# Thirty-eight passes written out without a loop, and the second attention's weights loaded in two halves

## The chip, the cores and the metric

One core of a Trainium2 chip runs the whole kernel. The metric is the device time of one execution in microseconds (us), as the median of several runs. The engines are TensorE (PE), VectorE (DVE), ScalarE (ACT), GpSimd (POOL) and SyncE (SP), which issues every DMA of this kernel. The sixteen DMA engines serve SP's one queue.

## The reference

A batch of 32 sequences of 256 tokens with 128 features goes through two transformer layers. Each half of a layer ends in a layer norm after the residual.

```
x = layernorm(x + L0_attn(x))   # 16 heads of 8, softmax over all 256 keys, distance bias
x = layernorm(x + L0_ffn(x))    # 8 experts, top 2 by softmax gate, plus one shared expert
x = layernorm(x + L1_attn(x))   # no full softmax: each token looks back at fixed offsets
x = layernorm(x + L1_ffn(x))    # 8 experts, one matrix each, top 2
```

The part that the change touches is the sum of the second attention, here with T = 256 and the offsets that are smaller than T:

```
for i, off in enumerate(OFFSETS):      # sorted, distinct, under 256: 16 of them
    vs = v shifted down by off
    out = out + attn[..., i] * vs      # attn has one weight per head, token and offset
out = (out * sigmoid(x @ w_gate + b_gate)) @ w_out + b_out
```

## The kernel before

**Passes.** The kernel is a software pipeline by hand. A sequence goes through the stages A1 and M (scores and their maxima, first attention), A2 and A3 (probabilities, output), B and B2 (first experts), C1 and C2 (second attention), D and D2 (second experts). Each stage lags by some passes (`LAG`, 0 to 6), so that in pass t the stage with lag k works on sequence t - k. There are 38 passes (t = 0 to 37). Every engine goes through its own list of steps (`ORDER`) in each pass, in that order, and waits on semaphores at each step. The `Steps` class counts them.

**The loop.** Passes 0 to 6 are written out. Passes 7 to 30 run in a loop of 12 rounds with two passes in its body, an odd one and an even one (`passes`, L286 to L295; `LOOP_FROM` is 7, `LOOP_TO` is 31). Passes 31 to 37 are written out again. So there are 11 jumps back, each between an even pass and the odd one after it: 8 to 9, 10 to 11, up to 28 to 29. The written-out passes 5 and 6 do the same work as those in the loop, but for the last experts' sums (D2), which begin in pass 6.

**The start of a pass.** On PE a pass begins with A1.qk (L423, L424). ACT turns its result into the highest of three bfloat16 parts (L668, L670). DVE makes the other two (L911, L915). SP stores the three (`d_parts<-parts`, L337) and loads them back as rows of the scores' stack with 12 DMAs (`stack<-d_parts`, L345 and L350), which wait for the stores. The score matmuls A1.S (L559, first of a pass: A1.S.0) need the stack. DVE takes the four norms' inverse roots together (N.root, L817 to L834). ACT applies them (L754), and PE transposes the results (L441).

**The weights of the second attention.** At the end of C1 the weights lie transposed in `wT`. SP stores them to DRAM (C1.dw, L374), then M.m (L384) goes out, and then SP loads `wb` with one DMA of 2048 KB (C1.wb, L380): each of the 128 partitions gets all 16 offsets of its head, 16 KB. In the next pass DVE multiplies offset pairs with shifted values (C2.pv.0 to .7, L923). Only pv.0 waits for the load. The pairs are taken in the order 0, 1, 4, 5, 2, 3, 6, 7 (`PV_ORDER`). DVE's list around them:

```
N.root.0 N.root.1 N.root.2 N.root.3 C2.pv.0 C2.pv.1 C2.pv.2 C2.pv.3
C2.pv.4 G.rank C2.pv.5 G.weigh C2.pv.6 C2.pv.7 A1.max.0 C2.add.0 ...
```

G.rank begins with a copy from PSUM (L845) of the gates' logits that PE makes at L458. POOL folds the sixteen products in two steps (C2.add, L1070): step 0 after the fourth product adds offsets 8 to 11 to 0 to 3, step 1 after the last adds 12 to 15 to 4 to 7. DVE folds the rest (L969, L974, L981) and applies the gate (L987).

**SP's list** of a pass:

```
A1.part.0 A3.x A1.part.1 A1.part.2 A1.rows.0 A1.rows.1 A1.rows.2 B.cT B.cb X.xT D.cT D2.out D.cb C1.dw M.m C1.wb
```

Of the kernel before, what the change touches and what calls it, by code (L numbers as in the profile page):

```python
# [6 lines left out]
B, T, D = 32, 256, 128  # L7
H, HD = 16, 8
# [30 lines left out]
LAST = max(LAG.values())  # L39
LOOP_FROM = LAST + 1  # L40
LOOP_TO = LOOP_FROM + (B - 1 - LOOP_FROM) // 2 * 2
Z_FIRST = 6
PV_ORDER = (0, 1, 4, 5, 2, 3, 6, 7)

# [22 lines left out]
        A1.part.0 A3.x A1.part.1 A1.part.2 A1.rows.0 A1.rows.1 A1.rows.2 B.cT B.cb X.xT D.cT D2.out D.cb C1.dw M.m  # L67
        C1.wb""",
}
# [31 lines left out]
def network(nc, A, out):  # L101
# [4 lines left out]
    with ctx:  # L106
# [139 lines left out]
        st_cB, ld_cB, st_cD, ld_cD = sem("st_cB"), sem("ld_cB"), sem("st_cD"), sem("ld_cD")  # L246
        st_w, ld_w, st_out = sem("st_w"), sem("ld_w"), sem("st_out")
        setup_dve, setup_act = sem("setup_dve"), sem("setup_act")
# [36 lines left out]

        def passes(eng, one):  # L286


            for t in range(LOOP_FROM):
                one(t, t % 2, t)  # L290
            with eng.Fori(0, (LOOP_TO - LOOP_FROM) // 2) as r:
                for u in range(2):
                    one(r * 2 + (LOOP_FROM + u), (LOOP_FROM + u) % 2, LOOP_FROM + u)
            for t in range(LOOP_TO, B + LAST):
                one(t, t % 2, t)  # L295
# [5 lines left out]
        def _(sp):  # L301
# [15 lines left out]
            def one(t, par, key):  # L317
                r = stages(t)
                for what, n in ORDER["sp"]:
# [3 lines left out]
                    if what == "X.xT" and (e := r["X"]) is not None:  # L323
                        sp.wait_ge(peA1.sem, peA1.count(e - 1, "v"))
                        sp.dma_start(xT[:], A["xT"][:, bass.ds(e * T, T)]).then_inc(ld_xT, 16)
                    if what == "A3.x":
                        if (e := r["A3"]) is not None:
                            sp.wait_ge(dveA3.sem, dveA3.count(e - 1, "res"))
                            sp.dma_start(x0[:], x_rows[:, bass.ds(e * TT, TT), :]).then_inc(ld_x, 16)
                    if what == "A1.part" and (e := r["A1"]) is not None:  # L330
# [39 lines left out]
                    if what == "C1.dw" and (e := r["C1"]) is not None:  # L370

                        sp.wait_ge(ld_w, dma_count(e - 1))
                        sp.wait_ge(actC1.sem, actC1.count(e, "wT"))
                        sp.dma_start(bass.AP(d_w.tensor, 0, [[T, 8], [NS * T, H], [8 * T, 2], [1, T]]),  # L374
                                     wT[:]).then_inc(st_w, 16)
                    if what == "C1.wb" and (e := r["C1"]) is not None:

                        sp.wait_ge(st_w, dma_count(e))
                        sp.wait_ge(dveC2.sem, dveC2.count(e - 1, "gt"))
                        sp.dma_start(wb[:].rearrange("p s n -> p (s n)"),  # L380
                                     bass.AP(d_w.tensor, 0, [[NS * T, H], [0, HD], [1, NS * T]])).then_inc(ld_w, 16)
                    if what == "M.m" and (e := r["M"]) is not None:
                        sp.wait_ge(actM.sem, actM.count(e, "mT"))
                        sp.dma_start(stack[par][ROW_M:ROW_M + 1, 0], mT[:]).then_inc(ld_m, 16)  # L384
                    if what == "D2.out" and (e := r["D2"]) is not None:
                        sp.wait_ge(actND.sem, actND.count(e, "nm", 1))
                        sp.dma_start(out_rows[:, bass.ds(e * TT, TT), :], xout[:]).then_inc(st_out, 16)

            passes(sp, one)
            sp.wait_ge(st_out, dma_count(B - 1))  # L390


        @block.tensor
        def _(pe):
# [14 lines left out]
            def one(t, par, key):  # L409
                if key == LOOP_FROM and not isinstance(t, int):  # L410
                    for b in last:
                        last[b] = (*last[b][:4], t - 1)
                if isinstance(t, int) and t == LOOP_TO:
                    for b in last:
                        last[b] = (*last[b][:4], LOOP_TO - 1)
                r = stages(t)
# [215 lines left out]

            passes(pe, one)


        @block.scalar
        def _(act):
# [129 lines left out]

            passes(act, one)


        @block.vector
        def _(dve):
# [116 lines left out]
            def one(t, par, key):  # L889
# [6 lines left out]
                for what, n in ORDER["dve"]:  # L896
# [20 lines left out]
                    if what == "C2.pv" and (e := r["C2"]) is not None:  # L917

                        if n == 0:
                            dve.wait_ge(ld_w, dma_count(e))  # L920
                            dve.wait_ge(actC1.sem, actC1.count(e, "v"))
                        p = PV_ORDER[n]
                        v.tensor_tensor(pv[:, 2 * p:2 * p + 2, :], wb[:, 2 * p:2 * p + 2, :], shifted(vC, p),  # L923
# [42 lines left out]
                    if what == "C2.add" and n == 0 and (e := r["C2"]) is not None:  # L966

                        dve.wait_ge(poolC2.sem, poolC2.count(e, "add", 1))
                        v.tensor_tensor(pv[:, 0:4, :], pv[:, 0:4, :], pv[:, 4:8, :], ALU.add).then_inc(dveC2.done("add", 0), 1)  # L969
                    if what == "N.root" and n == 1 and present:  # L970
# [77 lines left out]

            passes(dve, one)


        @block.gpsimd
        def _(pool):
# [4 lines left out]
            def one(t, par, key):  # L1058
                r = stages(t)
                odd = 1 - par  # L1060
                for what, n in ORDER["pool"]:
# [5 lines left out]
                    if what == "C2.add" and (e := r["C2"]) is not None:  # L1067

                        pool.wait_ge(dveC2.sem, dveC2.count(e, "pv", 4 * n + 3))
                        tt_(pv[:, 4 * n:4 * n + 4, :], pv[:, 4 * n:4 * n + 4, :], pv[:, 4 * n + 8:4 * n + 12, :],  # L1070
                            ALU.add).then_inc(poolC2.done("add", n), 1)
# [34 lines left out]

            passes(pool, one)

# [116 lines left out]
```

## Time and profile before

| | |
|---|---|
| median of 3 runs | 2006.53 us (1998.36 to 2018.55) |
| the profiled execution | 2014.43 us, of which 2012.6 us span |
| PE busy | 1601.7 us (80%) |
| DVE busy | 1334.9 us (66%) |
| ACT and POOL busy | 922.6 us, 917.0 us (46% each) |
| DMA moved | 214.15 MB, mean 106 GB/s |

No engine is busy throughout. The span runs from the first instruction to the last. In the rows below, a bracket at the end of a row of the timeline tells how long the engine was idle before the instruction and what ended that. "issue" means that it waited for nothing that the profile shows. Rows of SP are the moments at which DMAs were issued, not their transfer.

### The profile page before, as it was taken

The page shows a single profiled execution, that of the slowest core. Times are in us where ns is not written, and L with a number is a line of the kernel's source. Part 1 is how long each engine was busy: PE and PEld are TensorE (multiplying, and loading weights), DVE is VectorE, ACT ScalarE, POOL GpSimd, SP SyncE. Part 2 cuts the span into 40 slices and gives each one's busy share as a digit, 9 for nine tenths or more (in the row PEclk, how much of TensorE's full clock was granted, in tenths as well). Part 3 has the DMA queues.
Part 4 walks back from the last instruction along what each step waited for, and adds up shares of the span by engine and source line. Part 5 has one row for each costly group of instructions (what it writes and reads, how often), then busy time and mean ns, then how long its engine had stood idle before and what let it go on. Part 6 is the DMA issues. An engine that isn't in the chain of part 4 may idle for free.

```text
span 2012.6 us, 41817 instructions
## 1 busy us (share of the span) xinstructions
PE 1601.7 (80%) x12928; PEld 1209.2 (60%) x12928; DVE 1334.9 (66%) x3466; ACT 922.6 (46%) x1868; POOL 917.0 (46%) x772
## 2 busy tenths in 40 slices
PE   1788888887888888888878878888888888886633
PEld 1466666665666666566666656666666666664523
DVE  2456777776757767576767767677677767775543
ACT  1355444454545445454535545554455545543310
POOL 0014355455535554553555455355545554455542
PEclk9899989898989989899989898999899989998755
DMA  5334444354544434454443444444344445433321
GB/s 102 86 90 106 95 113 109 98 125 107 129 107 117 115 91 115 102 128 107 118 113 94 112 107 129 109 120 118 87 112 123 115 118 128 106 95 92 92 71 50
DMA packets 86025, 214.15 MB, mean 106 GB/s; under 512 B 11634, under 2 KB 68210, under 8 KB 68594
## 3 DMA queue, kind: packets, MB, share of 16 engines
q1 hardware_dynamic: 85844, 211.96, 42.6%
q8 instruction: 87, 1.43, 0.4%
q14 instruction: 94, 0.77, 0.2%
HBM read 185.97 MB, written 25.69 MB: 105 GB/s over the span
## 4 chain that ended last, share of the span: by engine, by line
PE 33%; issue 20%; POOL 15%; DMA 13%; DVE 10%; ACT 5%; SPq 3%; DVEq 0%; POOLq 0%; ACTq 0%
POOL prod L1079 7%; DMA d_parts<-parts 6%; DMA stack<-d_parts 5%; PE b L521 4%; PE bPV L542 3%; POOL h L1104 3%; DVE mx L1005 3%; PE bS L559 3%; PE bTU L571 3%; POOL prod L1095 3%; PE bTU L572 2%; PE b L580 2%; PE bTU L491 2%; POOL wb L1070 2%; PE bPV L510 2%
## 5 line engine op out<-in xcount | busy, mean ns | idle before, releaser
L1005 DVE TENSOR_REDUCE mx<-bS 128x2 f32<-128x512 f32 x512 | 337.0, 684 | 204.9 <-PE bS L562 202.4
L1079 POOL TENSOR_TENSOR prod<-kC,qC 128x512 f32<-128x512 f32 x256 | 363.7, 1451 | 142.2 <-ACT kC L683 142.2
L1104 POOL TENSOR_TENSOR h<-ub,gBcb 128x256 f32<-128x256 f32 x256 | 185.1, 729 | 422.3 <-DVE ub L1018 370.3
L1070 POOL TENSOR_TENSOR wb<-wb 128x1024 f32<-128x1024 f32 x64 | 162.6, 2541 | 417.3 <-DVE wb L923 417.3
L714 ACT ACTIVATE P<-bTU 128x512 f32<-128x512 f32 x512 | 276.8, 606 | 27.6 <-PE bTU L494 22.4
L559 PE MATMUL bS<-stack 96*128 96x256 bf16 x1024 | 232.8, 296 | 65.9 <-DMA stack<-d_parts 21.5
L723 ACT ACTIVATE sil<-bTU,b 128x256 f32<-128x256 f32 x288 | 136.7, 474 | 299.5 <-PE bTU L572 134.2
L571 PE MATMUL bTU<-x1T,w 128*128 128x256 f32 x576 | 203.5, 437 | 50.5 <-DVE h L1018 49.9
L491 PE MATMUL bTU<-stack 97*128 97x256 bf16 x1024 | 237.8, 284 | 4.9 <-ACT P L714 3.8
L494 PE MATMUL bTU<-dist,identh 128*128 128x128 f16 x1024 | 213.0, 226 | 0.0
L562 PE MATMUL bS<-dist,identh 128*128 128x128 f16 x1024 | 210.2, 233 | 0.0
L923 DVE TENSOR_TENSOR wb<-wb,vC 128x512 f32<-128x512 f32 x256 | 174.0, 731 | 45.1 <-DMA wb<-d_w 44.7
L559 PEld LDWEIGHTS bS<-stack 96*128 96x128 bf16 x1024 | 106.7, 104 | 154.2 <-DVE mx L1005 68.6
L572 PE MATMUL bTU<-x1T,w 128*128 128x256 f32 x576 | 185.3, 405 | 0.0
L1095 POOL TENSOR_TENSOR prod<-gDcb,x3T 128x512 f32<-128x512 f32 x128 | 160.6, 1267 | 34.1 <-DMA gDcb<-d_cD 34.1
L542 PE MATMUL bPV<-w,h 128*128 128x128 f32 x1152 | 154.0, 287 | 19.8 <-POOL h L1104 19.8
L521 PE MATMUL b<-ew,prod 128*128 128x128 f32 x1024 | 147.6, 299 | 17.1 <-POOL prod L1095 17.1
L542 PEld LDWEIGHTS bPV<-w,h 128*128 128x128 f32 x1152 | 143.7, 201 | 25.0 <-POOL h L1104 24.8
L521 PEld LDWEIGHTS b<-ew,prod 128*128 128x128 f32 x1024 | 135.5, 211 | 24.7 <-POOL prod L1095 14.3
L510 PE MATMUL bPV<-P,Vz 128*32 128x256 f32 x2048 | 148.0, 410 | 0.7 <-ACT P L714 0.7
L571 PEld LDWEIGHTS bTU<-x1T,w 128*128 128x128 f32 x576 | 94.1, 204 | 67.1 <-DVE h L1018 57.2
L491 PEld LDWEIGHTS bTU<-stack 97*128 97x128 bf16 x1024 | 106.1, 104 | 40.6 <-ACT P L714 26.4
(159 smaller groups left out, 2909.2 us busy)
## 6 DMA issues: line engine op xcount, KB each, us to landing
wb<-d_w SPq DMA_DIRECT2D x32, 2048.0 KB, 12.5
gBcb<-d_cB SPq DMA_DIRECT2D x32, 1024.0 KB, 4.8
gDcb<-d_cD SPq DMA_DIRECT2D x32, 1024.0 KB, 4.7
stack<-d_parts SPq DMA_DIRECT2D x288, 64.0 KB
stack<-d_parts SPq DMA_DIRECT2D x96, 192.0 KB
d_parts<-parts SPq DMA_DIRECT2D x96, 128.0 KB, 7.7
d_w<-wT SPq DMA_DIRECT2D x32, 256.0 KB
xT<-in_xT SPq DMA_DIRECT2D x32, 128.0 KB, 4.6
```

The lines of the kernel that those rows point to most:

```text
L491: mm(o[:, q], stack[odd][0:ROW_M + 1, 1, h, kt * 128:kt * 128 + 128], stack[odd][0:ROW_M + 1, 0, h, :], start=True, stop=False)
L494: i = mm(o[:, c], identh[:], dist[:, h, 0, :], start=False, stop=last_part)
L521: i = mm(b6[:, tt * 128:tt * 128 + 128], xs[:, x, tt * 128:tt * 128 + 128], ew[:, x, :], start=(x == 0), stop=(x == E - 1))
L542: i = mm(bPV[:, tt * 128:tt * 128 + 128], h9[:, x, tt * 128:tt * 128 + 128], w2[:, expert(x), :], start=False, stop=(x == E), skip_group_c ...
L559: mm(o[:, qt * T:qt * T + T], stack[par][0:ROW_M, 0, h, qt * 128:qt * 128 + 128], stack[par][0:ROW_M, 1, h, :], start=True, stop=False)
L571: mm(bAB[:, 0:T], w13[:, x, 0, :], x1T[:], start=True, stop=True)
L572: mm(bAB[:, T:2 * T], w13[:, x, 1, :], x1T[:], start=True, stop=True).then_inc(peB.done("ab", n), 1)
L714: act_f(P[k % 8][:].rearrange("p a b -> p (a b)"), bTU[turn_bank("ST", k)][:], ACT.Exp).then_inc(actA2.done("exp", k), 1)
L1005: v.tensor_reduce(mx[:, :, k], bS[k % 2][:].rearrange("p (a b) -> p a b", a=TT), op=ALU.max, axis=AX.X).then_inc(dveA1.done("max", k), 1)
L1079: tt_(prod[:, 2 * p:2 * p + 2, :], shifted(kC, p), qC[:].unsqueeze(1).to_broadcast([128, 2, T]), ALU.mult).then_inc(poolC1.done("prod", p), 1)
L1095: tt_(xs[:, 2 * i:2 * i + 2, :].rearrange("p x (t n) -> p x t n", t=TT), gD["cb"][:, :, 2 * i:2 * i + 2, :].rearrange("p t x n -> p x t n" ...
L1104: tt_(h9[:, n, :].rearrange("p (t n) -> p t n", t=TT), ub[n % 2][:].rearrange("p (t n) -> p t n", t=TT), gB["cb"][:, :, expert(n), :], ALU ...
```

## The change

1. The loop goes. `passes` writes all 38 passes out on each of the five engines. With it go the loop registers in DMA addresses and wait values, and the fix-ups of PE's bank bookkeeping at the loop's edges.
2. The load of `wb` is two DMAs of 1024 KB, offsets 0 to 7 (C1.wb.0) and 8 to 15 (C1.wb.1), issued one behind the other, each with its own semaphore. A partition's row is now 8 KB in each. DVE waits for the first half before pv.0 and for the second before pv.4.
3. `PV_ORDER` goes: the products are taken in the order 0 to 7. POOL's step 0 adds offsets 4 to 7 to 0 to 3, its step 1 adds 12 to 15 to 8 to 11, and DVE's first fold adds 8 to 11 to 0 to 3.
4. SP's wait before C1.dw is on the last product of the sequence before (pv 7), in place of the load of `wb`.

```diff
-        C1.wb""",
+        C1.wb.0 C1.wb.1""",
...
-        def passes(eng, one):
-
-
-            for t in range(LOOP_FROM):
-                one(t, t % 2, t)
-            with eng.Fori(0, (LOOP_TO - LOOP_FROM) // 2) as r:
-                for u in range(2):
-                    one(r * 2 + (LOOP_FROM + u), (LOOP_FROM + u) % 2, LOOP_FROM + u)
-            for t in range(LOOP_TO, B + LAST):
+        def passes(one):
+
+            for t in range(B + LAST):
                 one(t, t % 2, t)
...
-                        sp.wait_ge(ld_w, dma_count(e - 1))
+                        sp.wait_ge(dveC2.sem, dveC2.count(e - 1, "pv", 7))
                         sp.wait_ge(actC1.sem, actC1.count(e, "wT"))
...
-                        sp.wait_ge(st_w, dma_count(e))
-                        sp.wait_ge(dveC2.sem, dveC2.count(e - 1, "gt"))
-                        sp.dma_start(wb[:].rearrange("p s n -> p (s n)"),
-                                     bass.AP(d_w.tensor, 0, [[NS * T, H], [0, HD], [1, NS * T]])).then_inc(ld_w, 16)
+                        if n == 0:
+                            sp.wait_ge(st_w, dma_count(e))
+                            sp.wait_ge(dveC2.sem, dveC2.count(e - 1, "gt"))
+                        sp.dma_start(wb[:, 8 * n:8 * n + 8, :].rearrange("p s n -> p (s n)"),
+                                     bass.AP(d_w.tensor, 8 * n * T,
+                                             [[NS * T, H], [0, HD], [1, 8 * T]])).then_inc(ld_w[n], 16)
...
+                        p = n
+                        if n % 4 == 0:
+                            dve.wait_ge(ld_w[n // 4], dma_count(e))
                         if n == 0:
-                            dve.wait_ge(ld_w, dma_count(e))
                             dve.wait_ge(actC1.sem, actC1.count(e, "v"))
-                        p = PV_ORDER[n]
...
-                        v.tensor_tensor(pv[:, 0:4, :], pv[:, 0:4, :], pv[:, 4:8, :], ALU.add).then_inc(dveC2.done("add", 0), 1)
+                        v.tensor_tensor(pv[:, 0:4, :], pv[:, 0:4, :], pv[:, 8:12, :], ALU.add).then_inc(dveC2.done("add", 0), 1)
...
-                        tt_(pv[:, 4 * n:4 * n + 4, :], pv[:, 4 * n:4 * n + 4, :], pv[:, 4 * n + 8:4 * n + 12, :],
+                        tt_(pv[:, 8 * n:8 * n + 4, :], pv[:, 8 * n:8 * n + 4, :], pv[:, 8 * n + 4:8 * n + 8, :],
                             ALU.add).then_inc(poolC2.done("add", n), 1)
```

## Rows read from the trace of the kernel before

**Rows 1.** The page, its first line and PE's and DVE's busy time.

```profile
span 2012.6 us, 41817 instructions
...
PE 1601.7 (80%) x12928; PEld 1209.2 (60%) x12928; DVE 1334.9 (66%) x3466; ACT 922.6 (46%) x1868; POOL 917.0 (46%) x772
```

**Rows 2.** Waits: who waited for whom: us in total, times, longest us.

```profile
PE b L423 <- issue: 26.6, 6, 5.0
...
DVE n_v L817 <- issue: 14.7, 5, 4.1
...
PE bS L559 <- DMA stack<-d_parts: 21.5, 13, 7.2
...
DVE wb L923 <- DMA wb<-d_w: 44.7, 21, 6.8
...
DVE gL L845 <- PE b L458: 74.1, 30, 4.4
```

**Rows 3.** Timeline of PE, starts of passes 6, 7, 8, 9, 30, 31.

```profile
287.62 0.59 PE L423 MATMUL b<-xT,wqk 128*128 128x256 f32 x2
...
343.15 0.59 PE L423 MATMUL b<-xT,wqk 128*128 128x256 f32 x2
...
402.01 0.59 PE L423 MATMUL b<-xT,wqk 128*128 128x256 f32 x2
...
460.28 1.22 PE L423 MATMUL b<-xT,wqk 128*128 128x256 f32 x2 [4.00 <-issue]
...
1678.22 0.59 PE L423 MATMUL b<-xT,wqk 128*128 128x256 f32 x2
...
1733.41 0.59 PE L423 MATMUL b<-xT,wqk 128*128 128x256 f32 x2
```

**Rows 4.** Windows: us; busy PE, PEld, DVE, ACT, POOL; clock, DMA share, GB/s.

```profile
343.20:402.00 58.80, 51.38 (x405) 38.79 (x404) 40.30 (x106) 28.61 (x58) 28.71 (x24) 0.88 0.46 111
...
804.70:866.40 61.70, 51.72 (x406) 38.89 (x405) 40.27 (x107) 28.61 (x58) 28.82 (x24) 0.86 0.43 105
...
1564.50:1617.70 53.20, 46.01 (x406) 34.81 (x406) 40.93 (x106) 28.73 (x58) 28.87 (x24) 1.00 0.48 121
...
402.00:1678.20 1276.20, 1079.83 (x8889) 818.90 (x8888) 902.17 (x2311) 631.20 (x1276) 632.59 (x528) 0.93 0.45 112
```

**Rows 5.** Timeline, DVE and then PE, behind the jump back into pass 15.

```profile
818.75 0.17 DVE L817 TENSOR_SCALAR n_v<-n_mv 128x8 f32<-128x8 f32 x1 [4.12 <-issue]
...
823.17 0.47 PE L441 MATMUL b<-ident,x 128*128 128x128 f32 x1 [4.59 <-ACT x L754]
```

**Rows 6.** Timeline of SP from 860 to 900 us, start of pass 16.

```profile
867.78 0.56 SPq L380 DMA_DIRECT2D wb<-d_w  x1
869.13 0.37 SPq L337 DMA_DIRECT2D d_parts<-parts  x1
...
880.32 3.80 SPq L345 DMA_DIRECT2D stack<-d_parts  x9
```

**Rows 7.** Timeline of PE, pass 16: first score matmul.

```profile
893.66 0.28 PE L559 MATMUL bS<-stack 96*128 96x256 bf16 x1 [0.99 <-DMA stack<-d_parts]
```

**Rows 8.** Timeline of DVE, pass 16: five products, then the gate's logits.

```profile
880.12 3.10 DVE L923 TENSOR_TENSOR wb<-wb,vC 128x512 f32<-128x512 f32 x5 [1.19 <-DMA wb<-d_w]
884.95 0.19 DVE L845 COPY gL<-b 128x32 f32<-128x32 f32 x1 [1.73 <-PE b L458]
```

**Rows 9.** DMA issues: times, KB each, median us from issue to landing.

```profile
wb<-d_w SPq DMA_DIRECT2D x32, 2048.0 KB, 12.5
gBcb<-d_cB SPq DMA_DIRECT2D x32, 1024.0 KB, 4.8
...
stack<-mT SPq DMA_DIRECT2D x32, 8.0 KB, 2.2
```

**Rows 10.** Timeline of PE in pass 4, DVE in passes 33 and 34.

```profile
202.76 0.39 PE L559 MATMUL bS<-stack 96*128 96x256 bf16 x1 [0.16 <-DMA stack<-d_parts]
...
1904.95 3.10 DVE L923 TENSOR_TENSOR wb<-wb,vC 128x512 f32<-128x512 f32 x5 [2.58 <-DMA wb<-d_w]
...
1955.76 3.10 DVE L923 TENSOR_TENSOR wb<-wb,vC 128x512 f32<-128x512 f32 x5 [4.38 <-DMA wb<-d_w]
```

More of the change, by code:

```diff
@@ L246, in network @@
         st_cB, ld_cB, st_cD, ld_cD = sem("st_cB"), sem("ld_cB"), sem("st_cD"), sem("ld_cD")
-        st_w, ld_w, st_out = sem("st_w"), sem("ld_w"), sem("st_out")
+        st_w, ld_w, st_out = sem("st_w"), [sem(f"ld_w{n}") for n in range(2)], sem("st_out")
         setup_dve, setup_act = sem("setup_dve"), sem("setup_act")
@@ L324, in one @@
                         sp.wait_ge(peA1.sem, peA1.count(e - 1, "v"))
-                        sp.dma_start(xT[:], A["xT"][:, bass.ds(e * T, T)]).then_inc(ld_xT, 16)
+                        sp.dma_start(xT[:], A["xT"][:, e * T:e * T + T]).then_inc(ld_xT, 16)
                     if what == "A3.x":
@@ L328, in one @@
                             sp.wait_ge(dveA3.sem, dveA3.count(e - 1, "res"))
-                            sp.dma_start(x0[:], x_rows[:, bass.ds(e * TT, TT), :]).then_inc(ld_x, 16)
+                            sp.dma_start(x0[:], x_rows[:, e * TT:e * TT + TT, :]).then_inc(ld_x, 16)
                     if what == "A1.part" and (e := r["A1"]) is not None:
@@ L386, in one @@
                         sp.wait_ge(actND.sem, actND.count(e, "nm", 1))
-                        sp.dma_start(out_rows[:, bass.ds(e * TT, TT), :], xout[:]).then_inc(st_out, 16)
-            passes(sp, one)
+                        sp.dma_start(out_rows[:, e * TT:e * TT + TT, :], xout[:]).then_inc(st_out, 16)
+            passes(one)
             sp.wait_ge(st_out, dma_count(B - 1))
@@ L409, in one @@
             def one(t, par, key):
[L410 to L415, printed above, removed]
                 r = stages(t)
@@ L631, in one @@
                         i.then_inc(peM.done("mT"), 1)
-            passes(pe, one)
+            passes(one)
         @block.scalar
@@ L766, in one @@
                         nc.scalar.copy(mT[:], b7[:].bitcast(BF)[0:H, 0:T]).then_inc(actM.done("mT"), 1)
-            passes(act, one)
+            passes(one)
         @block.vector
@@ L1047, in one @@
                         v.tensor_scalar(mneg[:], mx[:], -1.0, None, ALU.mult).then_inc(dveM.done("neg"), 1)
-            passes(dve, one)
+            passes(one)
         @block.gpsimd
@@ L1105, in one @@
                             gB["cb"][:, :, expert(n), :], ALU.mult).then_inc(poolB.done("h", n - 1), 1)
-            passes(pool, one)
+            passes(one)
 def distance_tables():
```

3 lines of the change are left out of this document (removed).

## The prediction

> **What bounds the kernel now.** I read the page first. PE is busy 80% of the 2012.6 us, DVE 66%, and no engine is full [rows 1]. So the end is set by chains between engines and not by one engine's load, and I need to know what a pass costs and why passes differ. The starts of passes on PE give that. Passes 8 to 29 take 1276.2 us [rows 4], and 1276.2 / 22 = 58.0 us each. Four passes have no jump back at their start: pass 6 takes 343.15 - 287.62 = 55.5, pass 7 takes 58.9, pass 30 takes 55.2, and pass 8 takes 58.3 of which 4.0 is a stall at the jump that ends it, so 54.3 without [rows 3].
>
> The list of waits names the difference. PE stands still before the first matmul of a pass with the reason "issue" 26.6 us in 6 cases, and DVE before the norms' roots 14.7 us in 5 cases [rows 2]. 6 + 5 is 11, the number of jumps back. Around pass 15 the reader sees how such a stall goes on: DVE waits 4.12 us for nothing, the norms come late, and PE idles 4.59 us before it can transpose their results [rows 5]. That pass has a granted clock of 0.86 and takes 61.7 us. A pass with the clock at 1.00 takes 53.2 [rows 4]. So a stall can cost twice, once by itself and once by the clock that falls after PE's pause.
>
> Next I ask what limits a pass without a stall. In pass 16 the load of wb is issued at 867.78 and the store of the first parts at 869.13, behind it on the same queue. The rows of the stack can't be issued before 880.32 [rows 6]. PE waits the last 0.99 us before its first score matmul at 893.66 for the stack [rows 7]. The load of wb takes 12.5 us to land [rows 9], 867.78 + 12.5 = 880.3. So the first half of a pass is a chain of three DMA stages, and PE's own work is only about 1 us shorter. Over the run PE waits 21.5 us in 13 cases there [rows 2].
>
> **Part 1, the loop goes.** What goes is 11 jumps on five engines. The visible stalls are 26.6 + 14.7 = 41.3 us [rows 2]. I don't take that as the price, since a stall also moves the clock and since part of DVE's stall lies beside other work. I take the difference of whole passes: the mean of the four without a jump at their start is (55.5 + 58.9 + 54.3 + 55.2) / 4 = 56.0, against 58.0. That is 2.0 us in each of 22 passes, 45 us with the unrounded means (58.01 - 55.97). The two ways agree, which is why I trust the place. The ends: passes 6 and 7, which follow each other, average 57.2, and that gives only 22 x 0.8 = 18 us. The shortest pass of 53.2 gives 22 x 4.8 = 106 us, but it has no drop of the clock at all, so I hold it for out of reach.
>
> What it adds is code to fetch in a straight line. The written-out passes 6 and 30 to 31 show no stall at their starts [rows 3], so I cost it at nothing. The cover is that PE runs behind its queue. Without it a pass would stall about 4 us, as at a jump. The Trainium skill says the same (Runtime: NRT & Kernel Launch, section "Instruction fetch mechanics"): fetch ahead is sequential, and a taken branch to code outside the two pages at hand has to wait for a DMA. The trace agrees at the 11 jumps. By that page's sentence that runtime control flow costs and full unrolling is preferred, the gain would be all of the stalls; the sum above does not use it.
>
> **Part 2, the load in halves.** The bytes are the same. SP gets one more issue of 0.56 us [rows 6]. In pass 16 it would end at 867.78 + 2 x 0.56 = 868.9, before the store of the parts at 869.13, which waits for ACT. So it costs nothing there, with 0.2 us to spare. What lands when is not shown by any row. From below: gBcb, also with rows of 8 KB, lands 1024 KB in 4.8 us [rows 9], and two of these are 9.6, so 2.9 us sooner than now. From above: the second half pays a fixed part of its own, which a load of 8 KB shows as 2.2 us [rows 9], and waits 0.56 us to be issued. That would be 2.8 us later. I take 0 for the whole, because the source is the same (16 rows, each read by 8 partitions) and so the nearest row is wb itself.
>
> The first half then lands some 5 us before the second ((12.5 - 2.2) / 2, an estimate from [rows 9]), and pv.0 waits for nothing. In pass 16 that takes away 1.19 us on DVE. But the next thing DVE waits for is PE's logits, 1.73 us [rows 8], so it just waits there 1.2 us longer. This holds for the run: DVE waits 44.7 us for wb and right behind it 74.1 us for the logits [rows 2]. pv.4 needs the second half. It starts four products after pv.0, at 0.62 us each (3.10 / 5 [rows 8]) 2.5 us later, and so hides a second half that is up to 2.5 us late. POOL's first fold comes 1.2 us earlier, and then waits longer for the keys that ACT writes (its next step). In passes 4 and 5 pv.0 waits long, but PE starts its scores in pass 4 with the stack 0.16 us late [rows 10], so the stack caps the gain there. In passes 33 and 34, with no stack to load, pv.0 waits 2.58 and 4.38 us [rows 10]; of each at most the 2.5 us of four products goes. I take 5 us for both.
>
> **Part 3, the rest.** The order of products, the folds' addresses and SP's other wait change no size and no count. POOL's first fold still comes after the fourth product, its second after the last. The product pv 7 that SP now waits for is made long before wT is ready. All nothing.
>
> **Sum.** The profiled execution took 2014.4 us (span 2012.6 and 1.8 around it). 2014.4 - 45 - 5 = 1964.4. That execution lay 0.4% above the median of the three runs, so I scale by 2006.5 / 2014.4: 1957 us, 2.5% under the median of before.
>
> The skill's fit for one DMA is 2.0 us and the bytes at 436 per ns (DMA: Bandwidth & Descriptors, section "Anatomy of one DMA", written for GpSimd's path). It would make one load of 2048 KB 6.8 us and two loads that don't overlap 8.8 us, and the sum by it would be 2.0 us worse in each of 28 passes, 56 us. This trace has 12.5 us for that load, so the fit doesn't hold for it.
>
> **Rivals.**
> - *A, straight passes are no better than 6 and 7 together* (57.2). For it: pass 7 has no jump at its start, yet its clock is 0.88 and it takes 58.8 [rows 4]. Against it: pass 30 and pass 8. Gain 18 + 5: 1991.4, scaled 1984.
> - *B, the halves land sooner.* If wb lands 1 us earlier or more, the stack's wait of 0.99 us [rows 7] goes too, and PE's own order is next. 28 passes (4 to 31) have both loads: 28 more, 1936.4, scaled 1929. For it: gBcb's rate [rows 9]. Against it: another source pattern.
> - *C, the halves land later, and it ends slower.* Place: the store of the parts behind the two loads, in 28 passes. Price: up to 2.2 + 0.56 = 2.8 us each, and nothing hides it, since the stack already comes last [rows 7]. 28 x 2.8 = 78: 1964.4 + 78 = 2042.4, scaled 2034. It decides from 50 / 28 = 1.8 us of lateness on. The fit of the skill in the paragraph above is this rival's reason; its measured counterpart is the 2.2 us of a small load, and loads issued close together overlap that now (9 leave SP in 3.8 us [rows 6]).
> - *D, straight code doesn't take the stalls away*: they come back at other places of the 24 passes. Against it: the written-out passes. About 2002 to 2010.
>
> **Chances.** Forecast (1938 to 1978, a loop worth 25 to 65 us) 0.58; A 0.17; B 0.12; C 0.07; D 0.06. About 1% is what a measurement of this kernel can tell from no change, so the border is 1986. A lies on it, and I count half of it as faster. Faster: 0.58 + 0.09 + 0.12 = 0.79. Same: 0.08 of A, 0.05 of D, 0.02 of C = 0.15. Slower: 0.05 of C, 0.01 of D = 0.06. The range 1925 to 1992 holds the forecast, A and most of B. C and D lie outside.
>
> **What would show each step.** Right: no wait "issue" at the first matmul of a pass or at the norms' roots, passes 8 to 29 at 56 us on the mean, DVE's wait for wb near 0 outside the first passes, its wait for the logits grown by as much, PE's wait for the stack at 0 to 2 us. Wrong: the parts' store lands later than 14 us after the start of a pass (C), or sooner than 12 (B). The forecast fails most likely on the clock: if every straight pass drops to 0.88 as pass 7 does, the stalls are gone and half of the gain with them.

## The result, and the profile after

The changed kernel takes 1915.86 us (median of 4 runs, 1911.24 to 1918.87) against 2011.99 us for the kernel before in the same comparison (1998.36 to 2018.55, 4 runs). The ratio is 0.953, with a 95% interval of 0.947 to 0.959. That is 4.7% faster. The forecast was 1957, with 1925 to 1992 around it, so the direction was right and the gain was nearly twice the size: 96 us where 49 were expected.

The page first: the span, and the busy time of each engine with its share and its instructions.

```profile
span 1914.8 us, 36356 instructions
...
PE 1550.4 (81%) x12928; PEld 1176.4 (61%) x12928; DVE 1321.2 (69%) x3466; ACT 921.7 (48%) x1868; POOL 917.2 (48%) x772
```

The engines do the same work, instruction for instruction (compare the counts in [rows 1]). PE's busy time is 51 us less, at a granted clock of 0.935 of full speed over the span where before had 0.905. The rest of the gain is time in which PE stood still. Passes 8 to 29 are one window, from the first PE matmul of pass 8 to that of pass 30 (columns as in [rows 4]: us, then busy PE, PEld, DVE, ACT, POOL, then clock, DMA share, GB/s):

```profile
392.30:1588.00 1195.70, 1038.58 (x8889) 792.06 (x8888) 897.02 (x2311) 630.60 (x1276) 634.25 (x528) 0.96 0.48 120
```

1276.2 us in [rows 4] became 1195.7, so 80.5 of the 97.8 us between the two spans were won in these 22 passes, 54.35 us each in place of 58.01. The same windows laid over the ends give 227.6 to 215.9 us for passes 4 to 7, and 279.2 to 271.0 us from pass 31 to the end.

The list of waits has no "issue" any more at a pass's first matmul or at the norms' roots, where [rows 2] has 26.6 and 14.7 us. What it has instead (who waited for whom: us in total, times, longest us):

```profile
DVE gL L832 <- PE b L445: 85.8, 32, 3.7
...
PE bS L546 <- DMA stack<-d_parts: 60.8, 25, 7.9
```

PE's wait for the stack has grown from 21.5 us to 60.8. And DVE's wait for `wb`, 44.7 us before, is nearly gone. Its row in the list of instruction groups (out<-in, shape, count, then busy us and mean ns, then the idle time just before and what ended it):

```profile
L911 DVE TENSOR_TENSOR wb<-wb,vC 128x512 f32<-128x512 f32 x256 | 169.5, 711 | 8.7 <-DMA wb<-d_w 8.7
```

One pass shows what this means. In pass 20, which starts at 1046.56, SP issues both halves together, the store of the parts behind them, and the stack's rows 10.7 us after the first store (start us, us, line, times):

```profile
1047.85 1.18 SPq L372 DMA_DIRECT2D wb<-d_w  x2
1049.26 0.40 SPq L328 DMA_DIRECT2D d_parts<-parts  x1
...
1059.92 3.00 SPq L336 DMA_DIRECT2D stack<-d_parts  x9
```

PE is ready for its scores 1.90 us before the stack is:

```profile
1046.56 0.59 PE L410 MATMUL b<-xT,wqk 128*128 128x256 f32 x2
...
1074.23 0.28 PE L546 MATMUL bS<-stack 96*128 96x256 bf16 x1 [1.90 <-DMA stack<-d_parts]
```

So in this pass the chain of DMAs on SP's queue sets when the scores begin. In pass 16 DVE starts its products at once and waits for PE's logits instead, 2.76 us where [rows 8] has 1.19 for `wb` and 1.73 for the logits:

```profile
842.04 3.10 DVE L911 TENSOR_TENSOR wb<-wb,vC 128x512 f32<-128x512 f32 x5
847.90 0.19 DVE L832 COPY gL<-b 128x32 f32<-128x32 f32 x1 [2.76 <-PE b L445]
```

### The profile page after: what moved, and what is told of

Read it like the earlier page. It is cut to its first block, busy times and chain, and to the rows that moved or that the text cites. A ratio compares the mean times of both kernels' runs of the same rounds, so it can differ in the third digit from the quotient of the medians.

```text
span 1914.8 us, 36356 instructions
## 1 busy us (share of the span) xinstructions
PE 1550.4 (81%) x12928; PEld 1176.4 (61%) x12928; DVE 1321.2 (69%) x3466; ACT 921.7 (48%) x1868; POOL 917.2 (48%) x772
## 4 chain that ended last, share of the span: by engine, by line
PE 34%; DMA 30%; DVE 17%; issue 7%; SPq 6%; ACT 4%; POOL 3%; DVEq 0%; POOLq 0%; ACTq 0%
DMA d_parts<-parts 14%; DMA stack<-d_parts 13%; DVE mx L993 7%; PE bPV L529 5%; PE bS L546 4%; PE bTU L558 4%; SPq L336 4%; PE b L567 3%; PE bTU L559 3%; DVE wb L962 2%; DVE wb L957 2%; PE b L508 2%; PE bS L549 2%; DMA d_w<-wT 1%; POOL prod L1067 1%
## 5 line engine op out<-in xcount | busy, mean ns | idle before, releaser
L546 PE MATMUL bS<-stack 96*128 96x256 bf16 x1024 | 239.0, 301 | 97.6 <-DMA stack<-d_parts 60.8
L558 PE MATMUL bTU<-x1T,w 128*128 128x256 f32 x576 | 207.4, 445 | 41.2 <-DVE h L1006 40.8
L478 PE MATMUL bTU<-stack 97*128 97x256 bf16 x1024 | 227.0, 275 | 4.6 <-ACT P L701 3.6
L549 PE MATMUL bS<-dist,identh 128*128 128x128 f16 x1024 | 215.5, 237 | 0.0
L481 PE MATMUL bTU<-dist,identh 128*128 128x128 f16 x1024 | 206.5, 220 | 0.0
L559 PE MATMUL bTU<-x1T,w 128*128 128x256 f32 x576 | 188.1, 411 | 0.0
L911 DVE TENSOR_TENSOR wb<-wb,vC 128x512 f32<-128x512 f32 x256 | 169.5, 711 | 8.7 <-DMA wb<-d_w 8.7
L529 PE MATMUL bPV<-w,h 128*128 128x128 f32 x1152 | 148.3, 279 | 19.8 <-POOL h L1092 19.8
L529 PEld LDWEIGHTS bPV<-w,h 128*128 128x128 f32 x1152 | 136.9, 192 | 26.1 <-POOL h L1092 25.9
L497 PE MATMUL bPV<-P,Vz 128*32 128x256 f32 x2048 | 138.0, 387 | 0.7 <-ACT P L701 0.7
L559 PEld LDWEIGHTS bTU<-x1T,w 128*128 128x128 f32 x576 | 120.1, 209 | 19.5
L558 PEld LDWEIGHTS bTU<-x1T,w 128*128 128x128 f32 x576 | 96.0, 208 | 58.5 <-DVE h L1006 47.6
```

The source lines that it names most:

```text
L478: mm(o[:, q], stack[odd][0:ROW_M + 1, 1, h, kt * 128:kt * 128 + 128], stack[odd][0:ROW_M + 1, 0, h, :], start=True, stop=False)
L481: i = mm(o[:, c], identh[:], dist[:, h, 0, :], start=False, stop=last_part)
L529: i = mm(bPV[:, tt * 128:tt * 128 + 128], h9[:, x, tt * 128:tt * 128 + 128], w2[:, expert(x), :], start=False, stop=(x == E), skip_group_c ...
L546: mm(o[:, qt * T:qt * T + T], stack[par][0:ROW_M, 0, h, qt * 128:qt * 128 + 128], stack[par][0:ROW_M, 1, h, :], start=True, stop=False)
L549: i = mm(o[:, c], identh[:], dist[:, h, 0, :], start=False, stop=True)
L558: mm(bAB[:, 0:T], w13[:, x, 0, :], x1T[:], start=True, stop=True)
```

## The experiments

Eleven kernels ran, each timed beside the kernel before. They came in three groups with a median of before each (2008.42, 2017.62 and 2020.49 us), and the changed kernel was timed in a fourth (2011.99), so ratios are compared across groups and medians within one. The time of a pass is the window of passes 8 to 29 divided by 22. Windows, waits and spans come from one profiled execution of each kernel, ratios from all its runs. All of them compute the whole reference.

**The two parts apart.** The first takes the load in halves out of the changed kernel and leaves the loop gone; the other way round the second keeps the loop and has the halves. The third is the changed kernel, but DVE waits for both halves before its first product.

Straight passes only, against the changed kernel (against the kernel before, nothing but the loop is gone):

```diff
-        C1.wb.0 C1.wb.1""",
+        C1.wb""",
...
+                        sp.wait_ge(ld_w, dma_count(e - 1))
...
+                        sp.dma_start(wb[:].rearrange("p s n -> p (s n)"),
+                                     bass.AP(d_w.tensor, 0, [[NS * T, H], [0, HD], [1, NS * T]])).then_inc(ld_w, 16)
...
+                        p = PV_ORDER[n]
```

> The kernel before with its 38 passes written out and nothing else changed: one load of wb, the old order of products. Theory L (the loop is all of it, the forecast only mis-sized the gain of a straight pass): about 1920 us, passes 8 to 29 at 54.4 us as in the changed kernel. Theory H (the halves take part in every pass, because pv.0 starts at 12.2 us in a pass where it started at 13.7 behind the load): about 1957 us, passes at 56.0 us, DVE waiting for wb about 1 us in every pass.

Halves in the loop, against the kernel before (the load, the order and the folds as in the change, and SP waits for both loads where it waited for the one):

```diff
-                        sp.wait_ge(ld_w, dma_count(e - 1))
+                        for half in range(2):
+                            sp.wait_ge(ld_w[half], dma_count(e - 1))
```

> The kernel before, loop kept, with the load in two halves, the two semaphores and the new order of products (SP waits for both halves before C1.dw, since the wait on pv 7 isn't used here). Theory L: 2007 us, the 5 us of the first and last passes. Theory H: in each of the 12 even passes of the loop, in which pv.0 waits for wb now, 1.6 us or more go, so 1980 us or less.

Wait for both, against the changed kernel:

```diff
-                        if n % 4 == 0:
-                            dve.wait_ge(ld_w[n // 4], dma_count(e))
                         if n == 0:
+                            for half in range(2):
+                                dve.wait_ge(ld_w[half], dma_count(e))
```

> The changed kernel, but DVE waits for both halves before pv.0. The two DMAs, the order and the straight passes stay. Theory L: at most 5 us slower than the changed kernel, 1916 to 1921. Theory H: about 1950 us, since pv.0 is back at 13.7 us in a pass.

Straight passes alone took 1947.45 us, ratio 0.969 (0.962 to 0.976). Halves in the loop took 1991.16 us, 0.990 (0.982 to 0.998). The wait for both took 1936.29 us, 0.963 (0.956 to 0.971). None of the three came out as either theory had it: each lies between L (1920, 2007, at most 1921 us) and H (1957, at most 1980, 1950). The windows of the same 22 passes, one fence for each kernel in that order:

```profile
395.90:1605.30 1209.40, 1039.01 (x8890) 791.78 (x8889) 910.43 (x2311) 632.87 (x1276) 636.91 (x528) 0.97 0.49 119
```

```profile
396.90:1667.60 1270.70, 1067.48 (x8890) 813.90 (x8889) 898.77 (x2311) 630.56 (x1276) 631.74 (x528) 0.94 0.45 113
```

```profile
394.00:1591.80 1197.80, 1035.21 (x8890) 788.91 (x8889) 902.54 (x2311) 632.77 (x1276) 637.98 (x528) 0.97 0.49 120
```

A straight pass costs 54.97 us with one load, so the loop alone was worth (58.01 - 54.97) x 22 = 67 us by the profiles, and 61 by the medians (2008.42 - 1947.45). The halves add 32 us on top: (0.969 - 0.953) x 2012. By the profiled spans it is 1944.8 - 1914.8 = 30.0, of which 13.7 lie in passes 8 to 29, 6.0 in passes 4 to 7 (221.9 against 215.9 us) and 11.6 from pass 31 on (282.6 against 271.0); the other passes together lose 1.3. With the loop kept the halves bring 0.010 x 2012 = 20 us, and of these only 1276.2 - 1270.7 = 5.5 in passes 8 to 29.

The third kernel splits that again. It has the two DMAs but not DVE's early start, and in its profiled execution it is within 2.1 us of the changed kernel in passes 8 to 29, and within 0.3 us in passes 4 to 7 (216.2 against 215.9). So what the halves bring there comes from when the bytes land and not from when DVE begins. From pass 31 on it needs 279.9 us against 271.0, so the early start counts at the end. By the spans the early start is worth 1926.6 - 1914.8 = 11.8 us of the 30.0. But the profiled execution is the fastest of this kernel's four (1928.41 to 1941.22), and by the ratios it is (0.963 - 0.953) x 2012 = 20 us of the 32. Where the slower executions lose the difference isn't known. At the end there is no stack to load, and DVE waits (timeline of DVE near the end, first the changed kernel, then the one that waits for both):

```profile
1811.24 3.16 DVE L911 TENSOR_TENSOR wb<-wb,vC 128x512 f32<-128x512 f32 x5
...
1856.47 2.50 DVE L911 TENSOR_TENSOR wb<-wb,vC 128x512 f32<-128x512 f32 x4 [1.10 <-DMA wb<-d_w]
```

```profile
1869.15 3.10 DVE L911 TENSOR_TENSOR wb<-wb,vC 128x512 f32<-128x512 f32 x5 [5.51 <-DMA wb<-d_w]
```

When do the bytes land? The table has, for each of the 22 passes, the time from the pass's first PE matmul to the event, averaged, and a count of passes:

| us after the pass begins | before | straight only | wait for both | after |
|---|---|---|---|---|
| all of `wb` has landed | 13.09 | 14.04 | 13.49 | 13.46 |
| first product (DVE) | 14.45 | 14.07 | 13.57 | 12.20 |
| logits copied (DVE) | 20.01 | 18.07 | 18.07 | 18.06 |
| all of the stack has landed | 26.37 | 27.81 | 27.34 | 27.19 |
| first score matmul (PE) | 29.02 | 27.86 | 27.43 | 27.28 |
| passes (of 22) in which it starts within 0.3 us of the stack's landing | 9 | 22 | 20 | 21 |
| the pass | 58.01 | 54.97 | 54.45 | 54.35 |

(All of `wb` lands 1 us later into a straight pass than in before, because PE begins such a pass sooner.) Issued at 1.33 and 1.36 us into the pass, one load of 2048 KB lands at 14.04 and two of 1024 KB at 13.46, 0.58 us sooner, the first score comes 0.58 us sooner (27.86 and 27.28), and the pass is 0.62 us shorter. 22 x 0.62 = 13.7 us. In both kernels the first score follows the landing of all of `wb` by 13.8 us: the parts' store is behind the load in the queue, and the stack's rows are behind the store.

The stack is the last to arrive in nearly every straight pass, but not in the loop. There it is so in 9 of the 11 even passes and in none of the odd ones, in which it has been there for 2.2 to 8.0 us when PE gets to the scores. That fits the 5.5 us that the halves bring in the loop, where straight passes have 13.7.

**The collision of two engines.** The straight kernel with one load has one cost that I hadn't looked for. In pass 13 the timeline of DVE and then of POOL:

```profile
684.45 3.10 DVE L916 TENSOR_TENSOR wb<-wb,vC 128x512 f32<-128x512 f32 x5 [2.69 <-DMA wb<-d_w]
687.54 0.19 DVE L838 COPY gL<-b 128x32 f32<-128x32 f32 x1
687.88 2.16 DVE L846 TENSOR_TENSOR ggt<-gL 128x256 f32<-128x256 f32 x1
```

```profile
687.03 2.73 POOL L1063 TENSOR_TENSOR wb<-wb 128x1024 f32<-128x1024 f32 x1 [11.09 <-DVE wb L916]
```

The comparison of the gates takes 2.16 us while POOL's fold runs, and ends 0.3 us after it. Over the run, this group in before, straight only, wait for both, and after (busy us, mean ns):

```profile
L853 DVE TENSOR_TENSOR ggt<-gL 128x256 f32<-128x256 f32 x29 | 21.3, 735 | 0.0
```

```profile
L846 DVE TENSOR_TENSOR ggt<-gL 128x256 f32<-128x256 f32 x29 | 38.9, 1343 | 0.0
```

```profile
L840 DVE TENSOR_TENSOR ggt<-gL 128x256 f32<-128x256 f32 x29 | 24.8, 856 | 0.0
```

```profile
L840 DVE TENSOR_TENSOR ggt<-gL 128x256 f32<-128x256 f32 x29 | 12.0, 415 | 0.0
```

On the mean the same instruction costs 415 ns in the kernel whose fold is over by then (in the 22 passes it ends by 17.6 us and the logits come at 18.06), and 1343 where the two meet in every pass. The Trainium skill (SBUF — State Buffer, section "SBUF: two separate sides") says that a VectorE instruction with two SBUF inputs and a GpSimd instruction that reads SBUF lock a shared pair of ports against each other, each for its whole length. The trace agrees: 689.76 - 687.88 = 1.88 us of the fold were left when the comparison began, and it took 2.16.

To see what such a collision costs in time, the changed kernel gets one: POOL's fold waits until DVE has copied the logits.

```diff
+                        if n == 0 and r["G"] is not None:
+                            pool.wait_ge(dveG.sem, dveG.count(r["G"], "cp"))
```

> The changed kernel with POOL's first fold held back until the copy of the logits is done, so that it runs into the comparisons of G.rank. In the kernel with one load the first comparison took 1343 ns beside the fold, here 415. Both theories: the comparison takes 2 us or more again and the gates come 1.5 to 2 us later in a pass. Theory D': it delays the scores by as much, 22 x 1.5 = 33 us and more over the run: 1950 us. Theory S: PE waits for the stack in most passes anyway, with 1.45 us on the mean, so 1916 to 1930 us.

It took 1943.55 us, ratio 0.962 (0.955 to 0.970), some 18 us more than the changed kernel by the ratios and 28 by the spans (1943.3), between what the two theories had. The pass went to 55.42 us:

```profile
390.90:1610.20 1219.30, 1040.91 (x8890) 790.77 (x8889) 935.88 (x2311) 630.21 (x1276) 632.84 (x528) 0.97 0.48 118
```

DVE's busy time rose by 38.9 us with the same instructions. But the comparison isn't the one that was held, as expected. It is the small subtraction behind it, next to POOL's fold:

```profile
963.31 2.34 DVE L842 TENSOR_TENSOR gdl<-gL,gmx 128x32 f32<-128x32 f32 x1
```

```profile
962.98 2.62 POOL L1060 TENSOR_TENSOR wb<-wb 128x1024 f32<-128x1024 f32 x1 [11.94 <-DVE gL L832]
```

Here the gates come 2.7 us late (24.51 us into the pass against 21.78), PE's wait for the stack before its scores falls from 1.45 to 0.61 us a pass, and 1.07 us of each pass is left over. This kernel also does POOL's fold later, with all that follows from it, so the 18 to 28 us aren't the price of the collision alone. In the straight kernel with one load the gates come at 23.01 us, not half as late, and there the scores start with the stack's landing in all 22 passes. So the collision lies under the wait for the stack, and the 13.7 us of passes 8 to 29 go with the stack, which lands 0.62 us sooner (27.81 and 27.19). A run that takes the collision alone away from that kernel wasn't made.

**Which engine's jump costs.** The straight passes can be had engine by engine, since each engine runs its own list. A list names the engines that are written out, the others keep the loop: PE alone (shown here), then SP, ACT, DVE and POOL, then PE and DVE. These and the next are made from the kernel before, with its one load.

```diff
+        straight = []
...
+            if eng in straight:
+                for t in range(B + LAST):
+                    one(t, t % 2, t)
+                return
...
+            straight.append(pe)
             passes(pe, one)
```

The fourth shortens the loop on all engines to six rounds:

```diff
-LOOP_TO = LOOP_FROM + (B - 1 - LOOP_FROM) // 2 * 2
+LOOP_TO = LOOP_FROM + 12
```

> The kernel before with the passes written out on PE alone; the four other engines keep the loop. PE's stalls are 26.6 of the 41.3 us. If the price of the loop is PE's own stall and the clock behind it: 1965 to 1975 us, two thirds of the 61 us that straight passes on all engines gave. If any engine's jump sets the time of the pass, the stalls of DVE remain at all 11 jumps: 1990 us or more.

> The kernel before with the passes written out on SP, ACT, DVE and POOL; PE alone keeps the loop. Written out on PE alone, nothing was gained (ratio 0.997) and DVE stalled at all 11 jumps, 34.3 us. If each engine's stall covers the other's, the same holds the other way: PE stalls 4 to 5 us at all 11 jumps, 50 us, DVE's stall is gone, and the time is within 15 us of the kernel before. If only the jumps of engines other than PE count: 1950 us.

> The kernel before with the passes written out on PE and DVE; SP, ACT and POOL keep the loop. If these two engines' jumps are the whole price of the loop: about 1950 us, as with all five written out. If another engine's jump comes next (SP issues every DMA): a part of the 61 us stays, 1965 us or more, and a new wait stands at the jumps.

> The kernel before with 6 rounds of the loop (passes 7 to 18) in place of 12, the other passes written out: 5 jumps back in place of 11. Theory L: the gain goes by jumps, 6/11 of it: 2012 - 0.55 * 92 = 1961 us. Theory H: 6/11 of 45 us, so 1987 us. If only straight runs of many passes are fast, passes 19 to 30 show 54.4 us here and 7 to 18 show 58.

| straight on | ratio to before | passes 8 to 29, us | "issue" at the jumps |
|---|---|---|---|
| none (before) | 1 | 1276.2 | PE 26.6 in 6, DVE 14.7 in 5 |
| PE | 0.997 (0.994 to 1.001) | 1274.5 | DVE 34.3 in 11 |
| PE and DVE | 0.971 (0.966 to 0.976) | 1217.3 | none on either |
| all but PE | 0.976 (0.971 to 0.981) | 1227.6 | PE 24.5 in 6 |
| all | 0.969 (0.962 to 0.976) | 1209.4 | none |

PE straight alone gains nothing, as the second theory had it: the times of before return, and so do the stalls, on another engine. From the waits of that kernel, and of the one where only PE keeps the loop:

```profile
DVE n_v L823 <- issue: 34.3, 11, 4.3
```

```profile
PE b L429 <- issue: 24.5, 6, 4.3
```

In before each round had one visible stall, on PE or on DVE. With PE straight DVE stalls at all eleven jumps. So DVE's stall was there in every round, and where PE stalled too, it was hidden under PE's. Taking DVE's jump away as well brings the ratio from 0.997 to 0.971 and the window from 1274.5 to 1217.3 us. These 57 us are the price of DVE's jump: 57 / 11 = 5.2 us a jump, where the profile's own sum says 34.3 / 11 = 3.1. The rest shows on PE, whose busy time for the same matmuls is 1081.86 us in the one window, at a granted clock of 0.93, and 1037.29 in the other, at 0.97.

The other way round isn't the mirror image. With PE alone in the loop the expectation was stalls at all 11 jumps and no gain. PE stalled at 6, and 2.4% were gained, so that expectation failed. Against the kernel with all five written out, the jumps of PE alone cost 1227.6 - 1209.4 = 18 us of window, and those of SP, ACT and POOL together 1217.3 - 1209.4 = 8. These two are differences of single executions, and the intervals of the ratios overlap, so the 8 us aren't shown to be more than nothing. PE and DVE written out took 1959.02 us, between the 1950 and the 1965 of its two expectations, with no new wait at the jumps.

With six rounds the two states stand in one execution. Passes 8 to 18 hold five jumps, passes 19 to 29 none:

```profile
397.40:1034.70 637.30, 535.50 (x4445) 405.32 (x4444) 451.42 (x1155) 316.24 (x638) 316.86 (x264) 0.94 0.46 112
1034.70:1636.50 601.80, 517.48 (x4446) 394.49 (x4445) 454.81 (x1157) 316.52 (x638) 317.94 (x264) 0.97 0.49 119
```

That is 57.9 us and 54.7 us a pass, about the values of before and of straight only, as theory L had it. Of the difference of 35.5 us, 18.0 is PE's busy time, at a clock of 0.94 against 0.97 of its full 2.4 GHz for the same matmuls; the other half is time in which PE stood still. So the stall does cost twice in this execution, which is the fastest of the four. The median is 1986.47 us (1970.6 to 1997.3), ratio 0.989 (0.981 to 0.997). That is what H expected (1987) and not L (1961): the gain by all runs is about 22 us, where 6/11 of the 61 us would be 33.

**The queue.** If the landing of `wb` decides when the scores begin, then the second half, which DVE needs 2.5 us later anyway, should go behind the parts' stores. SP's list is changed, and its code takes the new step's name.

```diff
-        A1.part.0 A3.x A1.part.1 A1.part.2 A1.rows.0 A1.rows.1 A1.rows.2 B.cT B.cb X.xT D.cT D2.out D.cb C1.dw M.m
-        C1.wb.0 C1.wb.1""",
+        A1.part.0 A3.x A1.part.1 A1.part.2 C2.wb.1 A1.rows.0 A1.rows.1 A1.rows.2 B.cT B.cb X.xT D.cT D2.out D.cb C1.dw M.m
+        C1.wb.0""",
...
-                    if what == "C1.wb" and (e := r["C1"]) is not None:
+                    if what in ("C1.wb", "C2.wb") and (e := r[what[:2]]) is not None:
```

> The changed kernel with the load's second half issued in the next pass, behind the three stores of parts and ahead of the stack's rows. Theory S (the chain of load, store and stack sets when the scores begin, and the halves gain because they land 0.6 us sooner): the parts land about 4 us sooner, PE's wait of 1.45 us before the first score matmul goes, its own order is next at 25.8 us of a pass, and a pass takes about 52.9: 1885 us. Theory D (the halves gain because DVE starts sooner, the stack is only a bystander): 1916 us or more, because the second half lands later than now.

It took 1889.60 us (1886.13 to 1891.15), ratio 0.936 (0.930 to 0.942), the fastest of all. Under the changed kernel that is (0.953 - 0.936) x 2012 = 34 us by the ratios and 1914.8 - 1889.4 = 25 by the spans. A pass is 53.61 us. Theory D, which wanted 1916 us or more, is refuted.

```profile
387.70:1567.10 1179.40, 1030.31 (x8890) 785.20 (x8890) 905.11 (x2311) 630.89 (x1276) 627.86 (x528) 0.97 0.48 122
```

```profile
DVE wb L911 <- DMA wb<-d_w: 61.5, 33, 5.1
...
PE bS L546 <- DMA stack<-d_parts: 30.7, 19, 9.2
...
DVE gL L832 <- PE b L445: 24.9, 28, 3.7
```

DVE now waits 61.5 us for `wb`, which lands 16.57 us into the pass, and this costs nothing: it waits less for the logits behind it (24.9 us, not 85.8). PE's wait for the stack is halved. The chain over SP's queue was the one that counted, DVE's wait was not. The sooner store isn't passed on in full, though. On the mean of the 22 passes the first store of parts lands 8.90 us into the pass, 13.69 in the changed kernel, but all of the stack lands at 26.39, 27.19 there. So 4.8 us at the first link are 0.8 at the last, and the pass is 0.75 us shorter. The second half now stands in front of the stack's rows, which may be the reason; no run tests it.

**Smaller pieces.** The load in four DMAs of 512 KB, once all together and once with the last two behind the parts (SP's lists aren't shown).

```diff
-                        sp.dma_start(wb[:, 8 * n:8 * n + 8, :].rearrange("p s n -> p (s n)"),
+                        sp.dma_start(wb[:, 4 * n:4 * n + 4, :].rearrange("p s n -> p (s n)"),
...
-                        if n % 4 == 0:
-                            dve.wait_ge(ld_w[n // 4], dma_count(e))
+                        if n % 2 == 0:
+                            dve.wait_ge(ld_w[n // 2], dma_count(e))
```

> The changed kernel with the load in four DMAs of 512 KB (rows of 4 KB), a semaphore each, DVE waiting for each before its two products. Theory R (shorter rows land sooner, as the halves did by 0.6 us): 0.3 to 0.6 us more in each of 28 passes, 1900 to 1908 us. Theory F (each DMA has a fixed part, and SP's issues delay the first store by 1 us): the last quarter lands 0 to 1 us later, 1916 to 1940 us.

> The changed kernel with the load in quarters, the first two at the end of a pass as now, the last two behind the next pass's stores of parts. With the second half late (1889.6 us) DVE waits 2 us for it before its fifth product, at 16.6 us of a pass. A quarter needs half of that time, so that wait goes. If it is on the path: 0.3 us or more in each of 22 passes, 1880 us. If the stack still decides: 1885 to 1890 us.

Quarters together took 1908.14 us, ratio 0.946 (0.939 to 0.953), and land 12.83 us into the pass, again 0.6 us sooner than halves. But the stack lands only 0.18 us sooner (27.01), and the pass is 0.12 us shorter (1193.1 / 22 = 54.23). The time is at theory R's upper end (1908), but its interval overlaps that of the changed kernel, so the gain is not shown beyond doubt. With the last two late it is 1891.02 us, 0.937 (0.931 to 0.944), the same as with the late half:

```profile
DVE wb L911 <- DMA wb<-d_w: 4.8, 3, 2.6
...
PE bS L546 <- DMA stack<-d_parts: 33.0, 16, 6.3
```

DVE's wait for `wb` is nearly gone, the one for the stack is as long as with the late half, and so is the time. What is left in the pass is set elsewhere.

## Why the prediction was right and wrong

**What bounds the kernel: right.** The stalls at the jumps and the chain of three DMA stages were the two levers, and both moved the time. But the chain was read from pass 16, an even one. In the odd passes of the loop the stack came 2.2 to 8.0 us before PE needed it, so the chain was last in half of the passes before, and in nearly all only once the loop was gone. The forecast added the two parts as if they had nothing to do with each other.

**Part 1, right in place, too small: 45 us forecast, 61 to 67 measured.** The step that failed is "the mean of the four without a jump at their start". It made 56.0 of passes 6, 7, 8 and 30. In the straight kernel with one load the same four passes last 54.3, 56.9, 54.7 and 56.9 us, mean 55.7, while all 22 average 54.97. So 0.7 us of the 1.0 us by which the term was off come from four passes that are dearer than most, and 0.3 from single values, which scatter. I took "the two ways agree, which is why I trust the place" as support for the size as well: 41.3 us of visible stalls and 45 us of difference. They agree by chance. The visible stalls are a lower bound, because one engine's stall hides another's, as the kernel with PE straight shows, and because the clock falls behind them. The forecast had both reasons in words and still took the sum's nearness to 45 for support.

**Its added cost, nothing: right.** No "issue" wait at a pass's start appeared and the pass took 54.97 us, so rival D is refuted. But "the trace agrees at the 11 jumps" went too far: PE's stall and its fetch are there at 6 of them, as the last section shows. Rival A, passes no better than 57.2, is refuted too.

**Part 2, too small: 5 us forecast, 30 to 32 measured.** Two steps of it failed, and a third was wrong without a price that a run shows.

- "I take 0 for the whole", the landing. It is 0.58 us sooner, inside the range of 2.9 sooner to 2.8 later, and I had the price of it in rival B: the stack is the last to arrive, so what lands sooner starts the scores sooner. At 0 the term is nothing; at the measured 0.58 it would have been 22 x 0.58 = 13, and 13.7 were measured. That the 0.58 us go through in full is luck in part: of the 0.63 us by which quarters land sooner still, 0.18 reach the stack. B itself wanted 1 us or more. Rival C, the halves land later, is refuted by that number. The marks set for B and C, the parts' store landing before 12 or after 14 us, told neither: the first one lands at 13.69 us, and at 14.28 in the straight kernel with one load.
- "The stack caps the gain" in passes 4 and 5. The scores do wait for it, 6.09 us in pass 4 where [rows 10] has 0.16:

```profile
203.80 0.40 PE L546 MATMUL bS<-stack 96*128 96x256 bf16 x1 [6.09 <-DMA stack<-d_parts]
```

  Against the kernel before they begin 0.9 us sooner (27.41 us into the pass, 28.34 before), and the pass is 2.6 us shorter, 52.3 us after 54.9. So a cap on the start of the scores is none on the pass. But the early start isn't what the 6 us in passes 4 to 7 come from: the kernel that waits for both halves has 54.5 us in pass 4 and still 216.2 us for the four passes. From pass 31 on the halves brought 12 us (282.6 and 271.0), 9 of them by the early start (279.9 and 271.0), and not the 5 of two passes. Why it is worth more there than "at most the 2.5 us of four products" stays open.
- "POOL's first fold comes 1.2 us earlier, and then waits longer". It looked at POOL's own next wait and not at what DVE does beside the fold. The fold moved away from DVE's comparison of the gates: 735 ns before, 415 after, 9 us of DVE's busy time over the run. No run shows that this moved the end.

**DVE's wait for `wb` hidden behind the logits: right.** In straight passes the logits came at 18.06 us with the early start and at 18.07 without it. Between the straight kernel with one load and the changed one, DVE's wait for `wb` fell from 71.3 to 8.7 us and the one for the logits grew from 32.6 to 85.8, nearly as much. And PE's wait for the stack, forecast at "0 to 2 us", is 1.45 us a pass on the mean.

**The clock, the named danger, did not come.** The text said that straight passes might all drop to 0.88. The granted clock of the 22 passes rose from 0.93 to 0.96.

**The range.** Its low end of 1925 rested on "a loop worth 25 to 65 us" with the halves at 5, or B's 28 with the loop at 45. Both terms were forecast too low, and the range had no case with both high: 67 + 30 off 2014.4 is 1917, where the profiled execution took 1916.6.

## What to carry to other kernels

A sum of visible stalls is a lower bound where several engines stall at the same place: the worth of taking them away is that of whole passes in a stretch without them, and over as many passes as can be had, not four. Removing the stall of the engine that shows it most can bring nothing; write out the loop on every engine that meets the jump. And where a DMA queue is the chain that ends last, look at what stands in front of the urgent store: cutting a long load in two paid 30 to 32 us here (12 to 20 of them because the reader could start early), and issuing its second half behind that store paid 25 to 34 us more.

## What the runs showed of the hardware

**PE stalls at a jump in those rounds in which its queue fetches code.** The DMA queues of before in the round of passes 13 and 14 (690 to 805 us), where PE doesn't stall, and in the round of 17 and 18 (928 to 1046 us), where it does (queue, kind: packets, MB, share of 16 engines):

```profile
q14 instruction: 6, 0.05, 0.1%
```

```profile
q8 instruction: 9, 0.15, 0.6%
q14 instruction: 6, 0.05, 0.2%
```

In the first window the queue q8 has no line at all. The same holds for all eleven rounds: q8 moves 9 packets in each of the six rounds in which PE stalls at the start, and none in the five others. In the three other kernels with a jump on PE it is again 9 packets in each round with a stall (10 of 11 with the halves, 6 of 11 with PE alone in the loop, 2 of 5 with six rounds) and none in a round without. So it seems that PE's body of two passes is sometimes still at hand and sometimes not, and nothing here says what decides. In the changed kernel the same queue moves 103 packets over the run, in a straight line, and no pass starts with an "issue" wait.

**The kernel with the loop scatters more.** The kernel before ran from 1998 to 2031 us over all comparisons, 1.6% from end to end. Four runs of the changed kernel span 0.4%, of the straight one with one load 0.3%, of the late half 0.3%. But four runs each are few, and straight kernels with quarters span 0.7% and 1.0%, the halves in the loop 0.5%. That the loop is the cause isn't shown.

**The same bytes in more DMAs land sooner.** The same 2048 KB land 14.0 us into the pass as one DMA, 13.5 as two, 12.8 as four. Two things change together, the number of DMAs and the length of a partition's row, so these runs don't tell which counts. The Trainium skill has a rule that points the other way for DMA-bound transfers (SBUF — State Buffer, section "The DMA setup-cost knee": coalesce into the largest single transfer, because of a roughly fixed cost of each), and the measurement goes against it for this load. The Trainium skill's page Perfetto Trace Analysis, section "DMA Optimizations", says that splitting may let the whole finish sooner where the DMA engines are generally idle. This case, with a DMA share of 0.48, sides with that. Why the pieces land sooner stays open.
